# Where a transformer layer's output bias is added: GpSimd early, or VectorE in the last four expert groups

## The chip, the cores and the metric

One core of a Trainium2 chip runs the whole program. The metric is the device time of one launch in microseconds (us). The core has TensorE (PE), VectorE (DVE), ScalarE (ACT), GpSimd (POOL) and SyncE (SP), which here only issues transfers. Each engine works through its own instruction list in order, and the lists meet at semaphores.

## What the kernel computes

The input is x of 4 x 512 tokens and 256 channels. The result is x + attention(layernorm(x)) + experts(layernorm(x)), all in float32:

```
out  = einsum('bhqk,bkd->bhqd', softmax(q k^T * scale + window mask of 64), v)
attn = out.reshape(B, L, D) @ Wo + bo            # bo: 256 values, the bias this case is about
routed = einsum('ne,nef,efd->nd', comb, silu(x wg) * (x wu), wd)   # top 4 of 64 experts
shared = (silu(x swg) * (x swu)) @ swd
x = x + attn + routed + shared
```

The bias bo is a vector over the channels that is added to every token. It can be added at any place between x and the result.

## The kernel before

The 2048 tokens lie in 16 tiles (T) of 128, four for each of the four sequences (b). The stages, in the order of time:

1. **Head.** The four x blocks are loaded to `x_in[b]` (in the tile `wall`), normalized by DVE and ACT to `x_n[b]`, transposed and projected by PE. POOL rotates the queries of a tile (`rotate(T)`, four small operations, L1502 to L1508) and prepares the keys (`prepare_k`, L1478 to L1492).
2. **Attention turns, T = 0 to 15.** In each turn PE makes the scores of a tile twice (once to find the row maxima, which DVE reduces, L1110; once for the softmax), and the parts of three neighbouring tiles are in work at once. DVE also splits queries into bf16 parts (`leave`, L1104), copies keys (`near`, L1096), splits the maxima (L1119, L1121) and, in pieces set out by hand (`route_at`), works out the routing: top 4, ranks, the slots (L1230 writes `slot_i`). POOL sends each normalized tile four times to its experts' rows in DRAM (`scatter()`, L1518, an indirect DMA, 64 in all) with a rotation of tile T+4 in between. `SCATTERED_AT` says how many scatters a turn has: 4, in turns 12 and 13 six. From turn 1 on each scatter first waits for a step of PE.
3. **Base.** `add_x(T)` on DVE (L1155) adds x to the projected attention; the sum goes to DRAM (`base_d`). In the kernel before, x has had the bias added by then: `add_bias(b)` on POOL (L1575) adds `bo_sb` to the four tiles of `x_in[b]`, and `add_x` waits for it (`x_bo`).
4. **Expert groups, G = 0 to 31.** 127 blocks of 128 rows, four to a group. POOL copies the weights of each block's expert to a working buffer (L1545, up projection, buffers free when PE has used them; L1564, down projection). PE does `ups(G)` (L665), then `down(G-1)` (L690). Between them stand ACT's silu (L913) and DVE's `hidden(G)` (L1302, two products). `down(G)` begins only when all four down weights of its group are there. Results go to DRAM by ACT's copies (L926) and, in the last two groups, half by DVE (`copy_last_y`, L1309). The base rows are loaded back to `acc` in four parts of 512 KB (`load_base`), issued by SP in groups 24 to 27.
5. **Shared experts and sum.** PE does the shared experts (L604, L624). POOL fetches the four routed rows of each token (L1635, 64 indirect DMAs), DVE adds all (L1327, L1342) and SP stores the result.

## Time and profile before

| what | value |
|---|---|
| median of three runs | 370.13 us (370.11 to 371.2) |
| the profiled execution | 370.21 us |
| its span, first to last instruction | 368.9 us |
| PE busy | 336.3 us, 91% |
| POOL busy | 261.5 us, 71% |
| DVE busy | 252.4 us, 68% |
| ACT busy | 189.8 us, 51% |
| mean granted clock of TensorE | 0.986 of full |

The busy shares are means over stages with different limits. What a microsecond in one stage is worth is read from the chain of work that ended last, and from who waits for whom in that stage. 1.3 us of the execution's time lie outside the span.

### The profile page before, as it was taken

How to read it: one execution, taken by the hardware profiler on the slowest of the kernel's cores; microseconds unless marked ns; L12 is line 12 of the kernel's file. 1: busy time of each engine (PE TensorE's matmuls, PEld its weight loads, DVE VectorE, ACT ScalarE, POOL GpSimd, SP SyncE). 2: the span in 40 equal slices, each digit the busy share in tenths (PEclk: the TensorE clock that was granted, in tenths of full speed). 3: DMA queues.
4: the chain of work that ended last, by engine and by line, in shares of the span. 5: the costliest groups of instructions: out<-in, count | busy, mean ns of one | idle time of the engine just before them, and what ended most of it. 6: DMA issues, size and time to landing. Idle time of an engine off the chain costs nothing.

```text
span 368.9 us, 8678 instructions
## 1 busy us (share of the span) xinstructions
PE 336.3 (91%) x2710; PEld 250.6 (68%) x2711; DVE 252.4 (68%) x717; ACT 189.8 (51%) x359; POOL 261.5 (71%) x522
## 2 busy tenths in 40 slices
PE   6788589899898988899999999999999999999983
PEld 3676346566665565569999999999985466555572
DVE  4888899998898988645565464444444466677686
ACT  2595558898788876554555555555453111101100
POOL 6567988887777778525556657777773777777773
PEclk9999969999999999999999999999999999999998
DMA  8960233644494556679997883478985334444443
GB/s 246 231 159 4 72 109 114 199 159 147 143 267 156 155 173 182 176 223 221 348 320 226 273 267 115 173 239 276 294 278 180 107 114 132 130 124 129 128 142 114
DMA packets 73036, 66.81 MB, mean 181 GB/s; under 512 B 9053, under 2 KB 68701, under 8 KB 72993
## 3 DMA queue, kind: packets, MB, share of 16 engines
q1 hardware_dynamic: 66433, 49.30, 44.7%
q0 software_dynamic: 6144, 16.79, 14.4%
q8 instruction: 23, 0.38, 0.4%
q10 hardware_dynamic: 416, 0.18, 0.3%
q14 instruction: 20, 0.16, 0.1%
HBM read 36.78 MB, written 29.23 MB: 179 GB/s over the span
## 4 chain that ended last, share of the span: by engine, by line
PE 70%; DVE 16%; ACT 5%; issue 5%; DMA 2%; SPq 1%; DVEq 0%
PE bank L665 16%; PE bank L604 15%; PE bank L690 9%; PE bank L624 7%; PE bank L639 5%; PE bank L555 3%; PE bank L530 3%; DVE xall L1110 3%; PE bank L418 3%; PE bank L437 2%; DVE xall L1342 1%; PE bank L538 1%; DVE xall L1104 1%; DMA wdn<-edges 1%; DMA wall<-in_x 1%
## 5 line engine op out<-in xcount | busy, mean ns | idle before, releaser
L1635 POOL DMA_INDIRECT wall<-y_d,y_row x64 | 62.5, 977 | 26.0 <-issue 18.9
L1518 POOL DMA_INDIRECT xs_d<-spare,slot_i x64 | 64.7, 1012 | 19.2 <-issue 7.0
L1302 DVE TENSOR_TENSOR spare<-bank,spare 64x512 f32<-64x512 f32 (+1 forms) x64 | 44.1, 689 | 30.7 <-ACT spare L913 29.8
L665 PE MATMUL bank<-xall,spare 128*128 x508 | 63.9, 279 | 0.0
L665 PEld LDWEIGHTS bank<-xall,spare 128*128 128x128 f32 x508 | 59.4, 192 | 2.1
L1545 POOL COPY spare<-wall 128x256 f32 x127 | 48.0, 400 | 17.5 <-PE bank L665 9.8
L604 PE MATMUL bank<-xnT,xall 128*128 128x512 f32 x128 | 57.3, 594 | 0.0
L926 ACT ACTIVATE spare<-bank 128x512 f32<-128x512 f32 (+1 forms) x62 | 33.6, 593 | 28.7 <-PE bank L690 16.7
L604 PEld LDWEIGHTS bank<-xnT,xall 128*128 128x128 f32 x128 | 24.1, 190 | 25.1 <-issue 24.4
L872 ACT ACTIVATE xall<-bank 128x512 f32<-128x512 f32 x64 | 36.3, 599 | 8.1 <-PE bank L487 6.4
L889 ACT ACTIVATE xall<-bank 128x512 f32<-128x512 f32 x16 | 9.5, 597 | 59.6 <-PE bank L604 59.6
L864 ACT ACTIVATE xall<-bank 98x1024 bf16<-98x1024 bf16 x32 | 32.7, 1022 | 12.8 <-PE bank L437 11.5
L1342 DVE SCALAR_TENSOR_TENSOR xall<-wall,gate,xall 128x256 f32<-128x256 f32 x64 | 30.9, 485 | 2.3
L913 ACT ACTIVATE spare<-bank 64x512 f32<-64x512 f32 (+1 forms) x32 | 18.8, 587 | 25.1 <-PE bank L665 25.1
L624 PE MATMUL bank<-xall 128*128 128x256 f32 x128 | 29.7, 380 | 1.0 <-DVE xall L1327 1.0
L624 PEld LDWEIGHTS bank<-xall 128*128 128x128 f32 x128 | 24.3, 190 | 9.3 <-issue 5.3
L1172 DVE COPY xall<-bank 128x256 f32<-128x256 f32 x32 | 13.6, 424 | 24.8 <-PE bank L639 24.4
L855 ACT ACTIVATE xall<-xall 128x768 bf16<-128x768 f32 (+2 forms) x48 | 28.9, 625 | 1.6 <-DVE xall L1104 1.3
L1110 DVE TENSOR_REDUCE xall<-bank 128x4 f32<-128x316 f32 x64 | 27.9, 477 | 0.0
L487 PE MATMUL bank<-xall,wdn 128*128 128x256 bf16 x120 | 21.0, 278 | 6.3 <-ACT xall L872 4.2
L1316 DVE SCALAR_TENSOR_TENSOR xall<-xall,bank 128x512 f32<-128x512 f32 x16 | 11.0, 688 | 21.7 <-ACT xall L889 21.7
L1564 POOL COPY small<-wdn 128x128 f32 x24 | 7.0, 293 | 22.1 <-PE bank L690 21.9
(174 smaller groups left out, 640.8 us busy)
## 6 DMA issues: line engine op xcount, KB each, us to landing
y_d<-spare SPq DMA_DIRECT2D x31, 512.0 KB, 3.8
wall<-in_wg SPq DMA_DIRECT2D x16, 256.0 KB, 3.9
wall<-in_wu SPq DMA_DIRECT2D x16, 256.0 KB, 4.9
wdn<-in_wd SPq DMA_DIRECT2D x16, 256.0 KB, 4.6
spare<-xs_d SPq DMA_DIRECT2D x32, 128.0 KB, 3.4
small<-xs_d SPq DMA_DIRECT2D x32, 128.0 KB, 3.1
wall<-in_x SPq DMA_DIRECT2D x4, 512.0 KB, 5.5
base_d<-spare SPq DMA_DIRECT2D x16, 128.0 KB
```

Of the source, the lines that this page charges most:

```text
L604: ins = pe.matmul((gate_bank(i), up_bank(i))[half], wsh[:, c, half, ex, f0:f0 + P], xnT[:, c, g * GN:(g + 1) * GN], start=c == 0, stop=c = ...
L624: ins = pe.matmul(shared_bank(T), hs[T // GT % 2][:, k, t * P:(t + 1) * P], wshd[:, k, :], start=k == 0, stop=k == FC - 1)
L665: ins = pe.matmul(up_bank_of(G)[:, j * P:(j + 1) * P], wcur[i % NW][:, c * 2 * F:(c + 1) * 2 * F], x_half[c][:, bass.ds(o, P)], start=c == ...
L690: ins = pe.matmul(o[:, j * P:(j + 1) * P], hT[G % 2][rows64, j * P:(j + 1) * P], down_weights_of(G)[j][rows64, :], start=True, stop=True)
L872: act.activation(probs[n % 2][:, e * 512:(e + 1) * 512], bank[2 + e][:, :], ACT.Exp).then_inc(s["exp"], 1)
L926: act.activation(yb[G % 2][:, 0:n, half * P:(half + 1) * P], o[:, 0:n * P].rearrange("p (j d) -> p j d", d=P), ACT.Copy).then_inc(s["y_out ...
L1110: dve.tensor_reduce(maxf[T % 2][:, w * 8 + 4 * e:w * 8 + 4 * e + 4], bank[e][:, 0:4 * NEAR].rearrange("p (g n) -> p g n", g=4), AX.X, ALU.max,
L1302: ins = dve.tensor_tensor(hT[G % 2][half, 0:n], up_bank_of(G)[F:P, 0:n], sg[0:F, 0:n], ALU.mult)
L1342: dve.scalar_tensor_tensor(a, yk[:, T, k, :], gate[:, T, k:k + 1], a, ALU.mult, ALU.add).then_inc(s["sum"], 1)
L1518: pool.indirect_dma_start(out=xs_d, out_offset=bass.IndirectOffsetOnAxis(ap=slot_i[:, T, k:k + 1], axis=0), in_=x_n[b][:, t, :], in_offset ...
L1545: pool.tensor_copy(wcur[i % NW].rearrange("p (c g f) -> p c g f", c=NC, g=2), wall[:, bass.ds(o, WE)].rearrange("p (g c f) -> p c g f", c= ...
L1635: pool.indirect_dma_start(out=yk[:, T, k, :], out_offset=None, in_=of, in_offset=bass.IndirectOffsetOnAxis(ap=y_row[:, T, k:k + 1], axis=0 ...
```

## The change

POOL's 16 additions of the bias are gone, and with them DVE's wait for them. The bias is loaded later, by SP in group 18, to a row buffer that is free by then (`xrow[2]`), and DVE adds it to each of the four loaded parts of `acc` in groups 28 to 31, one operation of 128 x 1024 per group, behind `hidden(G)`. The fifth rotation, `rotate(4)`, moves from ahead of the scatters to between the four scatters of turn 0.

```diff
-    bo_sb = rt.take(D)
+    bo_late = xrow[2]
...
-    EXPERT_ROW, EXPONENTS = 13, 4
+    EXPERT_ROW, EXPONENTS, BIAS_AT = 13, 4, 18
...
         def add_x(T):
             dve.wait_ge(s["attended"], T + 1)
-            dve.wait_ge(s["x_bo"], T + 1)
...
+        def add_bias(b):
+            dve.wait_ge(s["bo"], 16)
+            dve.wait_ge(s[f"acc{b}"], 16)
+            a = acc[:, b * TPB:(b + 1) * TPB, :]
+            dve.tensor_tensor(a, a, bo_late.unsqueeze(1).to_broadcast([P, TPB, D]), ALU.add).then_inc(s["with_bo"], 1)
...
         def add_shared(T):
-            dve.wait_ge(s[f"acc{T // TPB}"], 16)
+            dve.wait_ge(s["with_bo"], T // TPB + 1)
...
+            if NGRP - B <= G < NGRP:
+                add_bias(G - (NGRP - B))
...
-        def add_bias(b):
-            pool.wait_ge(s["bo"], 16)
-            pool.wait_ge(s["normed"], (b + 1) * TPB // 2)
-            pool.wait_ge(s["normed_act"], (b + 1) * TPB // 2)
-            for t in range(TPB):
-                pool.tensor_tensor(x_in[b][:, t, :], x_in[b][:, t, :], bo_sb, ALU.add).then_inc(s["x_bo"], 1)
-                yield
...
         rotate_whole(3)
         prepare_k(3)
-        rotate_whole(4)
-        add_bias_whole(0)
-        add_bias_whole(1)
         slots = scatter()
         for T in range(NT):
-            if T == 0:
-                pieces = add_bias(2)
...
-                elif T == NT - TPB:
-                    pieces = add_bias(B - 1)
+            pieces = rotate(T + TPB) if T < NT - TPB else iter(())
...
-        sp.dma_start(bo_sb, bo.partition_broadcast(P)).then_inc(s["bo"], 16)
...
+            if G == BIAS_AT:
+                sp.wait_ge(s["g_T"], XB)
+                sp.dma_start(bo_late, bo.partition_broadcast(P)).then_inc(s["bo"], 16)
```

The instructions stand as follows. First POOL's list at the start of the scatters, before: the end of `prepare_k(3)`, `rotate(4)`, eight additions, then scatters with the additions of the third block between them.

```order
L1492 CAST xall<-xall 128x4x16
L1502 TENSOR_TENSOR xall<-xall,cf 128x128
L1504 TENSOR_TENSOR xall<-xall,cf 128x128
L1506 TENSOR_TENSOR xall<-xall 128x16x4
L1508 TENSOR_TENSOR xall<-xall 128x16x4
L1575 TENSOR_TENSOR wall<-wall,wdn 128x256 x8
L1518 DMA xs_d<-spare,slot_i 8192x256
L1575 TENSOR_TENSOR wall<-wall,wdn 128x256
L1518 DMA xs_d<-spare,slot_i 8192x256
```

The same place in the changed kernel, whose lines are numbered a little otherwise (L1525 is the scatter, L1509 to L1515 the rotation):

```order
L1499 CAST xall<-xall 128x4x16
L1525 DMA xs_d<-spare,slot_i 8192x256
L1509 TENSOR_TENSOR xall<-xall,cf 128x128
L1525 DMA xs_d<-spare,slot_i 8192x256
L1511 TENSOR_TENSOR xall<-xall,cf 128x128
L1525 DMA xs_d<-spare,slot_i 8192x256
L1513 TENSOR_TENSOR xall<-xall 128x16x4
L1525 DMA xs_d<-spare,slot_i 8192x256
L1515 TENSOR_TENSOR xall<-xall 128x16x4
```

So the first scatter stands right behind `prepare_k(3)`, and 12 additions are gone from here. Next POOL's list in turns 12 to 15, before: the last rotation, then the remaining scatters with the four additions of the fourth block.

```order
L1508 TENSOR_TENSOR xall<-xall 128x16x4
L1518 DMA xs_d<-spare,slot_i 8192x256
L1575 TENSOR_TENSOR wall<-wall,wdn 128x256
L1518 DMA xs_d<-spare,slot_i 8192x256 x4
L1575 TENSOR_TENSOR wall<-wall,wdn 128x256
L1518 DMA xs_d<-spare,slot_i 8192x256 x2
L1575 TENSOR_TENSOR wall<-wall,wdn 128x256
L1518 DMA xs_d<-spare,slot_i 8192x256 x4
L1575 TENSOR_TENSOR wall<-wall,wdn 128x256
L1518 DMA xs_d<-spare,slot_i 8192x256 x5
```

After the change sixteen scatters stand there with nothing between them. Last, DVE's list in groups 28 to 31 and behind them, in the changed kernel (L1301 is `hidden`, L1308 `copy_last_y`, L1315 the first operation of the shared experts):

```order
L1301 TENSOR_TENSOR spare<-bank,spare 64x512 x30
L1325 TENSOR_TENSOR xall<-xall,spare 128x1024
L1301 TENSOR_TENSOR spare<-bank,spare 64x512 x2
L1325 TENSOR_TENSOR xall<-xall,spare 128x1024
L1301 TENSOR_TENSOR spare<-bank,spare 64x512 x2
L1325 TENSOR_TENSOR xall<-xall,spare 128x1024
L1308 COPY spare<-bank 128x4x128
L1301 TENSOR_TENSOR spare<-bank,spare 64x384 x2
L1325 TENSOR_TENSOR xall<-xall,spare 128x1024
L1308 COPY spare<-bank 128x3x128
```

The rows L1325 are the new additions; the third stands ahead of the first `copy_last_y`, the fourth ahead of the second. Nothing else on DVE has moved, and PE's list is the same in both.

## Rows read from the trace of the kernel before

**Rows 1.** The chain that ended last, its last long piece: start us, us, what

```profile
355.30 7.19 PE bank L624 x32
```

**Rows 2.** The chain that ended last, 28 to 70 us

```profile
38.15 0.88 DVE xall L1104
...
40.93 0.78 DVE slot_i L1230
41.71 0.84 DVE wdn L1096
...
47.39 0.77 DVE slot_i L1230
...
49.40 0.67 DVE xall L1121
...
51.96 1.91 PE bank L530 x16
```

**Rows 3.** POOL's timeline: start us, us, engine, line, what

```profile
38.02 5.78 POOL L1575 TENSOR_TENSOR wall<-wall,wdn 128x256 f32<-128x256 f32 x8
...
47.36 0.74 POOL L1575 TENSOR_TENSOR wall<-wall,wdn 128x256 f32<-128x256 f32 x1
...
49.28 0.74 POOL L1575 TENSOR_TENSOR wall<-wall,wdn 128x256 f32<-128x256 f32 x1
```

**Rows 4.** Single lines of DVE: duration ns min/median/max, first and last start us

```profile
L1104 DVE TENSOR_TENSOR xall<-xall x32: 409/416/991, 19.6 to 140.7; 128x256 f32<-128x256 f32 x32
L1096 DVE COPY wdn<-xall x16: 310/328/909, 27.1 to 149.7; 98x640 bf16<-98x640 bf16 x16
L1121 DVE TENSOR_TENSOR xall<-xall x16: 174/214/659, 36.0 to 154.2; 128x16 bf16<-128x16 f32 x16
L1230 DVE TENSOR_SCALAR slot_i<-wdn x2: 765/770/776, 40.9 to 47.4; 128x32 int32<-128x32 f32 x2
```

**Rows 5.** Timelines of POOL and DVE, a scatter beside a small DVE operation

```profile
57.03 0.98 POOL L1518 DMA_INDIRECT xs_d<-spare,slot_i  x1 [0.17 <-issue]
57.40 0.59 DVE L1119 CAST xall<-xall 128x16 bf16<-128x16 f32 x1
```

**Rows 6.** Timelines of DVE and POOL in turns 13 and 14

```profile
137.82 0.70 DVE L1104 TENSOR_TENSOR xall<-xall 128x256 f32<-128x256 f32 x1
140.68 0.73 POOL L1575 TENSOR_TENSOR wall<-wall,wdn 128x256 f32<-128x256 f32 x1
140.71 0.99 DVE L1104 TENSOR_TENSOR xall<-xall 128x256 f32<-128x256 f32 x1
```

**Rows 7.** Timelines of POOL and DVE, a 128 x 1024 addition beside a rotation

```profile
67.55 1.41 POOL L1504 TENSOR_TENSOR xall<-xall,cf 128x128 f32<-128x128 f32 x1
67.48 1.23 DVE L1248 TENSOR_TENSOR wdn<-wdn,small 128x1024 f32<-128x1024 f32 x1
```

**Rows 8.** Timelines of PE, DVE and POOL, groups 29 and 30

```profile
273.53 1.16 PE L690 MATMUL bank<-spare 64*128 64x128 f32 x16
271.19 1.40 DVE L1302 TENSOR_TENSOR spare<-bank,spare 64x512 f32<-64x512 f32 x2 [1.35 <-ACT spare L913]
269.80 0.40 POOL L1545 COPY spare<-wall 128x256 f32 x1
271.19 1.00 POOL L1564 COPY spare<-wdn 128x128 f32 x4
```

**Rows 9.** The DMA view: a transfer's issues, KB each, median us to landing

```profile
xall<-base_d SPq DMA_DIRECT2D x4, 512.0 KB, 6.8
```

**Rows 10.** Timeline, the end of the last group

```profile
280.97 0.75 PEld L690 LDWEIGHTS bank<-spare 64*128 64x128 f32 x12 [0.85 <-DVE spare L1302]
281.99 0.56 DVE L1309 COPY spare<-bank 128x384 f32<-128x384 f32 x1 [1.07 <-PE bank L690]
```

**Rows 11.** Windows: us, busy us (count) of PE, PEld, DVE, ACT, POOL, granted clock, DMA share, GB/s

```profile
48.00:49.00 1.00, 1.00 (x4) 0.39 (x2) 0.97 (x4) 0.44 (x1) 0.83 (x2) 0.50 0.24 86
...
53.00:54.00 1.00, 0.97 (x11) 0.15 (x4) 0.81 (x4) 1.00 (x3) 0.80 (x3) 0.50 0.57 169
```

More of the change, by code:

```diff
@@ L116 @@
     "stats moments var scaled rs normed biased route member totals_read rank_read slots rows "
-    "q_left diag wslice shifted gate k_out k_near o_out max mpart max_out rden a_tok ah hs h y_out_dve gT_dve expert_read with_x based sum "
-    "v_fill fill prep roped k_split weights down_weights x_bo "
+    "q_left diag wslice shifted gate k_out k_near o_out max mpart max_out rden a_tok ah hs h y_out_dve gT_dve expert_read with_x with_bo based sum "
+    "v_fill fill prep roped k_split weights down_weights "
 ).split() + [f"fetched{T}" for T in range(NT - 1)] + [f"last_fetched{k}" for k in range(TOPK)]
@@ L1331, in sum_up @@
             if T in SUM_FIRST:
-                dve.wait_ge(s[f"acc{T // TPB}"], 16)
+                dve.wait_ge(s["with_bo"], T // TPB + 1)
             else:
@@ L1568, in gpsimd @@
         pool.wait_ge(s["c32"], 16)
-        def add_bias(b):
-            pool.wait_ge(s["bo"], 16)
-            pool.wait_ge(s["normed"], (b + 1) * TPB // 2)
-            pool.wait_ge(s["normed_act"], (b + 1) * TPB // 2)
-            for t in range(TPB):
-                pool.tensor_tensor(x_in[b][:, t, :], x_in[b][:, t, :], bo_sb, ALU.add).then_inc(s["x_bo"], 1)
-                yield
-        def add_bias_whole(b):
-            for _ in add_bias(b):
-                pass
         def rotate_whole(T):
@@ L1593, in gpsimd @@
         prepare_k(3)
-        rotate_whole(4)
-        add_bias_whole(0)
-        add_bias_whole(1)
         slots = scatter()
         for T in range(NT):
-            if T == 0:
-                pieces = add_bias(2)
-                for i in range(SCATTERED_AT(T)):
-                    next(slots)
-                    next(pieces)
-            else:
-                if T < NT - TPB:
-                    pieces = rotate(T + TPB)
-                elif T == NT - TPB:
-                    pieces = add_bias(B - 1)
-                for i in range(SCATTERED_AT(T)):
+            pieces = rotate(T + TPB) if T < NT - TPB else iter(())
+            for i in range(SCATTERED_AT(T)):
+                if T > 0:
                     if i < 2:
@@ L1616, in gpsimd @@
                         pool.wait_ge(s["weighted"], QB * (T - 1) + min(i, 4) - 2)
-                    next(slots, None)
-                    if T < NT - TPB or i in (0, 4):
-                        next(pieces, None)
+                next(slots, None)
+                next(pieces, None)
         for _ in slots:
```

## The prediction

> **What bounds the kernel now.** I read the chain that ended last first, because the page's busy shares hide which engine counts in which stage. From about 160 us to 362 us the chain is PE almost without a gap; its last long piece is a run of 32 products of 7.19 us [rows 1]. In that stretch work taken off POOL gains nothing by itself; what matters is only whether something new makes PE wait. From 28 to 70 us it is otherwise. There DVE's routing steps stand on the chain [rows 2], and so do a few of them again in turns 13 and 14. All POOL additions that the change removes lie in these two stretches. Every engine behind them is paced by turns, with no transfer found waiting at a fixed time, so a microsecond gained there should reach the end.
>
> The next view is the timeline of POOL beside that of DVE. POOL is not waited for in the early stretch, yet it costs time. Eight additions run back to back from 38.02 us, 0.72 us each [rows 3], and the DVE operations under them are long: L1104 takes 0.88 us on the chain, L1230 0.78, L1096 0.84 [rows 2]. The view of single lines gives their usual lengths, 0.416 us for L1104, 0.328 for L1096, 0.174 at the least for L1121 [rows 4]. L1230 runs twice and takes 0.77 both times, each time with an addition of POOL under it, so its free length is not in the trace. The ends tell the mechanism. Additions at 0.7225 us each from 38.02 have an end at 40.91 and one at 41.63; L1230 starts at 40.93 and ends at 41.71, just behind the second. The single additions at 47.36 and 49.28 [rows 3] end at 48.10 and 50.02, and the DVE operations over them end at 48.16 and 50.07 [rows 2]. DVE waits until POOL's instruction is done. The two engines hold something in turns, not side by side.
>
> The Trainium skill (SBUF — State Buffer, "Who interferes with whom") has a rule for that: the two engines share one pair of ports to the memory, held as a lock for a whole instruction, and a VectorE operation with two inputs in SBUF is in its way only against a GpSimd instruction that reads there. The trace agrees with the lock for whole instructions.
>
> **Part by part, the gain.** (a) *Turn 0, 38 to 42.5 us.* After the change POOL has nothing between the end of `prepare_k(3)`, 36.6 us, and the first scatter, which must wait for L1230. So three waits go: L1104 0.88 - 0.42 = 0.46; L1230 0.78 less its free length; L1096 0.84 - 0.33 = 0.51. For L1230 the nearest free row is L1121's 0.174 (128 x 16, also a tiny operation), which gives 0.60. Its bounds are 0 (all of its 0.77 is its own) and 0.60. The sum is 1.57; I take 1.5, as L1096 now meets the start of the first scatter. Low end 0.7, high end 1.6. ACT does not catch it: its table load in this stretch hangs on PE's transposes, which L1104 also holds up.
>
> (b) *Turn 1, 45 to 51 us.* The second L1230 and L1121 lose the additions under them: 0.60 and 0.67 - 0.17 = 0.50, together 1.1. But scatters come in their place, since POOL reaches turn 1 about 5 us earlier. A scatter also holds DVE: L1119 takes 0.59 beside one instead of some 0.17 [rows 5], so 0.4 a hit. I take half, 0.5, between 0 (both meet one again) and 1.1. The skill's rule, taken at its word, frees L1121 (two inputs) from scatters that only write descriptors, and would put this term at 0.7; the sum goes by the row.
>
> (c) *Turns 12 to 14.* L1104 is at 0.70 and at 0.99 with additions of the fourth block under it [rows 6], against 0.42: 0.28 + 0.57 = 0.85. I take 0.8, between 0.2 (the scatters that move forward collide in their place) and 1.0.
>
> (d) *At nothing:* the moved rotation. `rotate(4)` ends at some 47 us instead of 38, and is needed by ACT only in turn 2, after 51 us; the cover is 4 us. Also the wait `x_bo` in `add_x`, which had always been met; and the 128 KB load that leaves the head of SP's queue. In group 18 SP issues that load ahead of one y store: less than a microsecond of SP's time, which idles about 2 us in each group there; behind it only y stores are queued, for which ACT has a group's time.
>
> The gain is 1.5 + 0.5 + 0.8 = 2.8 us, with ends at 0.9 and 3.7.
>
> **The price.** (e) Four additions of 128 x 1024 on DVE. The same shape took 1.23 us [rows 7]. DVE's own time hides them: between `hidden(29)`, done at 271.19 + 1.40 = 272.59, and `hidden(30)` about 3.1 us after 271.19 there are 1.7 us. What they wait for is there: the `acc` parts are issued four groups ahead, 12 us, against 6.8 us to landing [rows 9]. But they have both inputs in SBUF and hold POOL, whose weight copies feed PE. The row for it is L1504, which took 1.41 us instead of 0.41 under L1248 [rows 7]: held until the addition ends. I follow the first two on POOL's timeline. The addition of group 28 is due at 269.83, just after POOL's copy at 269.80 [rows 8] has begun, so it starts at about 270.15 and ends at 271.3. POOL's two remaining copies for `ups(30)` come at 271.3 and 271.65, needed by PE in `ups(30)`, the 2.0 us ahead of 273.53, at 272.5 and 273.0: no stall. The four down weights of group 29, before at 271.19 to 272.19 [rows 8], now begin at 272.0, one each 0.24 us. The fourth is due at 272.71, and the second addition of DVE is due at 272.7. If DVE is first, that copy ends at 274.1, while `down(29)` is due at 273.53 [rows 8] and waits for all four: a PE stall of 0.6. If POOL is first, nothing. In group 30 the same meeting falls at 275.6 to 275.7 and has 0.5 us at stake. In group 31 POOL has finished. I put 0.5 for the two, between 0 and 1.2.
>
> (f) In group 31 `hidden` ends as PE needs it, PE waits for it [rows 10], and nothing is put ahead of it. The addition behind it, 280.92 to 282.1, delays the last y copy, due at 281.99 [rows 10], by 0.1 us, and with it the fetches of the routed rows, which POOL issues nearly without a pause up to the end. I put 0.1.
>
> The sum against the execution's own time: 370.21 - 2.8 + 0.6 = 368.0 us, 0.6% below the median of 370.13, from which the execution differs by 0.08.
>
> The Trainium skill (VectorE: DVE Perf Modes, fp32 formula for an add of two tensors) gives (1024 + 151)/0.96 = 1224 ns for the new addition, an estimate; the trace agrees with its 1.23 us. Its lock for whole instructions speaks against this change: by it POOL stands still for nearly 4 x 1.2 us in the groups, and only POOL's slack keeps this from PE.
>
> **Rivals.** *The scatters take the additions' place* (0.17). The DVE waits of turns 1 and 12 to 14 stay, and L1230 is slow by itself. For it: rows 5, and no free L1230 in the trace. Against it: in turn 0 no scatter can start before L1230. Gain 0.9, price 0.6: 369.9, within what can't be told.
>
> *The clock does not fall* (0.13). The granted clock is 0.50 at 48 us and still at 53, the lower of TensorE's levels, 1.2 against 2.4 GHz [rows 11], after PE had stood idle for much of 40 to 48 us waiting for DVE. With the waits gone it may stay up. PE's 16 products of L530 took 1.91 us at that level [rows 2], about 0.95 too long; with the transposes ahead of them it is some 1.3 us, of which DVE, busy at 0.8 to 0.97, lets perhaps 1.0 through: 367.0 us. Against it: PE still idles most of those microseconds.
>
> *The clock falls at a worse time* (0.09), the case on the slow side. If the fall comes in turns 2 to 4, where PE is busy nearly all the time, and lasts twice the present six microseconds, it costs up to half its length, 6 us, less the 1.3 of the present one and what DVE would hide: some 4 us, and 368.0 + 4.0 = 372.0 us. It decides against the change from about 3.3 us of added cost, that is, 6.6 us more of half clock over work bound by PE. Against it: the early idling shrinks, so nothing asks for more.
>
> *The additions hold POOL more than worked out* (0.08): both meetings lost and the gain at its middle, 368.7 us, still faster.
>
> *The forecast* has 0.53, with its own range 367.2 to 368.8.
>
> **How the numbers follow.** A measurement of this kernel tells about 0.3%, 1.1 us: faster is below 369.0. Forecast, high clock and lost meetings give 0.74, of which some spills over 369.0; I put faster at 0.70, same at 0.20, slower at 0.10. The range reaches up to the first rival and down to the second: 366.7 to 369.9.
>
> **What would show it.** L1104 of turn 0 at 0.42 us, the first L1230 at about 0.2, the first scatter near 41 us and not 44; turn 1's L1230 and L1121 shorter on average by a half; L1104 of turn 14 at 0.42; the four additions at 1.2 us each in groups 28 to 31, POOL's copies beside them late by about 1 us, and a gap ahead of `down(29)` of 0 or 0.6. I am wrong if L1230 stays at 0.77 with no POOL instruction under it, if the interval to 160 us shrinks by less than 1 us, or if PE's run through the last four groups grows by more than 1.2 us.

## The result, and the profile after

The changed kernel takes 366.2 us, the median of 15 runs (363.9 to 369.2), beside 370.2 us for the kernel before on the same chip (15 runs, 368.4 to 372.6). The ratio is 0.989, with an interval of 0.987 to 0.991: 4.0 us or 1.1% faster. The forecast was 2.1 us less, with a range of 0.2 to 3.4 us less. The direction was right and the size too small: the result lies outside the range.

The profiled execution of the changed kernel took 367.16 us, 3.05 us less than that of before. It is slower than the median by about 1 us. From its start to turn 0 it is 0.6 us behind that of before (the first pair of L1110 reductions of turn 0's routing starts at 35.41 us, before at 34.82), where the change only takes the bias load away; with that load back, in `head_load`, the pair starts at 35.27. Net of that, the part that the change touches is 3.6 us shorter, near the difference of the medians. The lines moved by one: L1230 of before is L1229 now, the scatter is L1525, the rotation L1509 to L1515, the new addition L1325, the weight copies on POOL L1552 and L1571.

First the page's busy time and clock.

```profile
PE 336.9 (92%) x2711; PEld 251.1 (69%) x2711; DVE 252.1 (69%) x721; ACT 190.2 (52%) x359; POOL 252.2 (69%) x506
PEclk9999969999999999999999999999999999999998
```

The timeline of DVE in turns 0 and 1 (start us, us, engine, line), which answers to [rows 2]:

```profile
38.45 0.42 DVE L1104 TENSOR_TENSOR xall<-xall 128x256 f32<-128x256 f32 x1
...
40.77 0.18 DVE L1229 TENSOR_SCALAR slot_i<-wdn 128x32 int32<-128x32 f32 x1
40.86 0.32 DVE L1096 COPY wdn<-xall 98x640 bf16<-98x640 bf16 x1
...
43.99 0.67 DVE L1104 TENSOR_TENSOR xall<-xall 128x256 f32<-128x256 f32 x1 [1.51 <-ACT xall L855]
...
46.44 0.35 DVE L1229 TENSOR_SCALAR slot_i<-wdn 128x32 int32<-128x32 f32 x1
...
47.90 0.17 DVE L1121 TENSOR_TENSOR xall<-xall 128x16 bf16<-128x16 f32 x1
...
52.50 0.69 DVE L1136 COPY xall<-bank 128x512 f32<-128x512 f32 x1 [0.86 <-PE bank L530]
```

The three operations that waited for POOL in turn 0 have their free lengths: 0.42, 0.18 and 0.32 us. L1096 now ends at 41.18 us instead of 42.55. The last row is new: in turn 1 DVE waits 0.86 us for PE. It waits for the 16 products of L530, which took 1.91 us before [rows 2] and take 1.86 now, from 50.57 us on. The windows say that the clock still falls, only earlier (the last three columns are the granted clock, the DMA share and GB/s):

```profile
46.00:47.00 1.00, 0.53 (x4) 0.47 (x4) 0.96 (x6) 0.91 (x2) 0.81 (x3) 0.50 0.07 29
...
50.00:51.00 1.00, 1.00 (x14) 0.63 (x16) 0.93 (x3) 0.85 (x3) 1.00 (x1) 0.50 0.34 111
```

It is back at 1.00 from 53 us on.

POOL's timeline, which answers to [rows 3]: nothing stands between `prepare_k(3)` and the first scatter, and the rotation's pieces lie between the scatters.

```profile
41.84 1.19 POOL L1525 DMA_INDIRECT xs_d<-spare,slot_i  x1 [4.58 <-DVE slot_i L1229]
...
43.64 1.02 POOL L1525 DMA_INDIRECT xs_d<-spare,slot_i  x1 [0.17 <-issue]
...
46.40 0.34 POOL L1513 TENSOR_TENSOR xall<-xall 128x64 f32<-128x64 f32 x1
```

Set one beside the other: L1229 at 46.44 to 46.79 us and the rotation at 46.40 to 46.74 end together. The rotation now holds DVE where it stands. L1104 at 43.99 has become longer too, 0.67 us instead of 0.43. It ends at 44.66 with the scatter that began at 43.64, behind which the next piece of the rotation stands.

DVE in turn 13, which answers to [rows 6]:

```profile
136.07 0.42 DVE L1104 TENSOR_TENSOR xall<-xall 128x256 f32<-128x256 f32 x1
...
138.26 0.18 DVE L1121 TENSOR_TENSOR xall<-xall 128x16 bf16<-128x16 f32 x1
138.35 0.42 DVE L1104 TENSOR_TENSOR xall<-xall 128x256 f32<-128x256 f32 x1
```

Both L1104 are free, and so is an L1121 that took 0.61 us before, which the forecast hadn't counted. Last, the expert groups. DVE and POOL in groups 28 and 29:

```profile
265.07 1.40 DVE L1301 TENSOR_TENSOR spare<-bank,spare 64x512 f32<-64x512 f32 x2 [1.67 <-ACT spare L913]
266.50 1.44 DVE L1325 TENSOR_TENSOR xall<-xall,spare 128x1024 f32<-128x1024 f32 x1
268.14 1.40 DVE L1301 TENSOR_TENSOR spare<-bank,spare 64x512 f32<-64x512 f32 x2 [0.20 <-ACT spare L913]
269.57 1.34 DVE L1325 TENSOR_TENSOR xall<-xall,spare 128x1024 f32<-128x1024 f32 x1
271.21 1.40 DVE L1301 TENSOR_TENSOR spare<-bank,spare 64x512 f32<-64x512 f32 x2 [0.30 <-ACT spare L913]
```

```profile
266.47 2.42 POOL L1552 COPY spare<-wall 128x256 f32 x4 [0.37 <-PE bank L665]
268.84 1.00 POOL L1571 COPY spare<-wdn 128x128 f32 x4
...
269.55 0.29 POOL L1571 COPY spare<-wdn 128x128 f32 x1
```

PE, down products of group 29 and the first wide product behind group 30's (before they started at 273.53 [rows 8] and 274.62 us):

```profile
264.33 1.16 PE L690 MATMUL bank<-spare 64*128 64x128 f32 x16
...
270.48 1.16 PE L690 MATMUL bank<-spare 64*128 64x128 f32 x16
271.57 1.98 PE L604 MATMUL bank<-xnT,xall 128*128 128x512 f32 x4
```

From `down(27)` to `down(29)` it is 6.15 us, before too (267.38 to 273.53), and 1.09 us on to L604 in both. PE has no gap: in this execution the four additions cost it nothing. POOL's copies are held (four L1552 in 2.42 us), but it has the time. It was close, though. The row at 269.55, asked for alone, is the last of the four copies of down weights at 268.84. `down(29)` needs it, and it began 0.02 us ahead of the addition at 269.57. The experiments show executions in which the addition came first. The lead of 3.05 us at 271.57 is the same as at PE's last long piece, 352.25 us instead of 355.30 [rows 1].

The offsets give the change by stages. Start to turn 0: 0.59 later. At the end of the first L1096: 1.37 earlier, so turn 0 gave 1.96. At 62 us: 1.52, so turn 1 gave 0.15. It stays between 1.5 and 1.55 through turn 11. At the pair of turn 15: 2.86, and behind the turns 3.05, so turns 12 to 15 gave 1.5. Behind that: nothing. Together 3.6 us.

### The profile page after: what moved, and what is told of

Its sections match the earlier page's. It is cut to its first block, busy times and chain, and to the rows that moved or that the text cites. A ratio compares the mean times of both kernels' runs of the same rounds, so it can differ in the third digit from the quotient of the medians.

```text
span 365.8 us, 8665 instructions
## 1 busy us (share of the span) xinstructions
PE 336.9 (92%) x2711; PEld 251.1 (69%) x2711; DVE 252.1 (69%) x721; ACT 190.2 (52%) x359; POOL 252.2 (69%) x506
## 4 chain that ended last, share of the span: by engine, by line
PE 76%; DVE 12%; ACT 6%; issue 4%; POOL 1%; DVEq 0%; POOLq 0%
PE bank L665 16%; PE bank L604 15%; PE bank L690 10%; PE bank L624 7%; PE bank L639 5%; PE bank L530 4%; PE bank L555 4%; DVE xall L1110 4%; PE bank L418 3%; PE bank L437 3%; PE bank L406 2%; PE bank L487 2%; DVE xall L1347 1%; PE bank L538 1%; ACT xall L872 1%
## 5 line engine op out<-in xcount | busy, mean ns | idle before, releaser
L1525 POOL DMA_INDIRECT xs_d<-spare,slot_i x64 | 64.6, 1010 | 27.0 <-PE bank L487 7.2
L1301 DVE TENSOR_TENSOR spare<-bank,spare 64x512 f32<-64x512 f32 (+1 forms) x64 | 44.1, 689 | 27.9 <-ACT spare L913 27.0
L1552 POOL COPY spare<-wall 128x256 f32 x127 | 49.9, 416 | 17.9 <-PE bank L665 10.0
L604 PE MATMUL bank<-xnT,xall 128*128 128x512 f32 x128 | 57.3, 594 | 0.0
L604 PEld LDWEIGHTS bank<-xnT,xall 128*128 128x128 f32 x128 | 24.1, 190 | 25.1 <-issue 24.4
L1110 DVE TENSOR_REDUCE xall<-bank 128x4 f32<-128x316 f32 x64 | 27.9, 477 | 0.0
L1315 DVE SCALAR_TENSOR_TENSOR xall<-xall,bank 128x512 f32<-128x512 f32 x16 | 11.0, 688 | 21.5 <-ACT xall L889 21.5
L1571 POOL COPY small<-wdn 128x128 f32 x24 | 7.0, 293 | 22.9 <-PE bank L690 22.8
```

Source lines behind the costliest of these rows:

```text
L604: ins = pe.matmul((gate_bank(i), up_bank(i))[half], wsh[:, c, half, ex, f0:f0 + P], xnT[:, c, g * GN:(g + 1) * GN], start=c == 0, stop=c = ...
L1110: dve.tensor_reduce(maxf[T % 2][:, w * 8 + 4 * e:w * 8 + 4 * e + 4], bank[e][:, 0:4 * NEAR].rearrange("p (g n) -> p g n", g=4), AX.X, ALU.max,
L1301: ins = dve.tensor_tensor(hT[G % 2][half, 0:n], up_bank_of(G)[F:P, 0:n], sg[0:F, 0:n], ALU.mult)
L1525: pool.indirect_dma_start(out=xs_d, out_offset=bass.IndirectOffsetOnAxis(ap=slot_i[:, T, k:k + 1], axis=0), in_=x_n[b][:, t, :], in_offset ...
L1552: pool.tensor_copy(wcur[i % NW].rearrange("p (c g f) -> p c g f", c=NC, g=2), wall[:, bass.ds(o, WE)].rearrange("p (g c f) -> p c g f", c= ...
```

## The experiments

There were eighteen runs. In fourteen of them (all but the one group of four) every execution, those of the kernel before too, took 384 to 400 us, but for one of 652 us. In their profiles ScalarE stood still three or more times, for up to 16 us, nearly always in the shared-expert stage, which no edit touches; there only profiles and large differences are read. One row of the first run, of ACT in the shared-expert stage, where the idle time ended with nothing that the trace holds:

```profile
337.51 1.08 ACT L889 ACTIVATE xall<-bank 128x512 f32<-128x512 f32 x2 [14.38 <-remote]
```

### The halves of the change, undisturbed

One group of four on one chip, three rounds: the changed kernel again, its two halves, and the rotation put back. The kernel before took 370.92 us there (22 executions; `late_all` and `rotate_ahead` have 6 each, `early_late` 11, `last_late` 12). `early_late` is the changed kernel with the fourth block's additions left on POOL in turns 12 to 14:

```diff
+            elif T == NT - TPB:
+                pieces = pool_bias(B - 1)
...
-            if NGRP - B <= G < NGRP:
+            if NGRP - B <= G < NGRP and G - (NGRP - B) in (0, 1, 2):
```

`last_late` leaves the first three blocks' additions on POOL, ahead of the scatters and between them in turn 0, with `rotate(4)` ahead of them as before, and adds only the fourth block late:

```diff
+        rotate_whole(4)
+        for b in range(2):
+            for _ in pool_bias(b):
+                pass
...
+            if T == 0:
+                pieces = pool_bias(2)
...
+            if NGRP - B <= G < NGRP and G - (NGRP - B) in (3,):
```

`rotate_ahead` is the changed kernel with only the rotation moved back:

```diff
+        rotate_whole(4)
         slots = scatter()
...
-            pieces = rotate(T + TPB) if T < NT - TPB else iter(())
+            pieces = rotate(T + TPB) if 0 < T < NT - TPB else iter(())
```

> The changed kernel on a third chip. In the two sets before, all kernels took 385 to 396 us, the kernel before too, with pauses of ScalarE of 14 us each in the shared experts that end on nothing in the trace; there its gain over the kernel before was not seen. Where such pauses are absent, port theory: 3.6 us under the kernel before (ratio 0.990). Where they are there, a difference of 1 to 3 us between kernels is not told apart, whatever the theory.

> Additions of sequences 0 to 2 on VectorE late, those of sequence 3 on GpSimd in turns 12 and 13. Without pauses: 2.1 us under the kernel before (port theory, turns 0 and 1 alone), or 3.6 us (order theory: what counts is when the scatters start).

> Additions of sequence 3 alone on VectorE late. Without pauses: 1.5 us under the kernel before (port theory, turns 12 to 14 alone), or under 0.5 us (order theory). The earlier run of this kernel had L1231 at 0.77 us and L1097 at 0.91 us in turn 0 as the kernel before, which the port theory needs, and I expect both again.

> The changed kernel with the fifth rotation put back ahead of the scatters. I costed the move at nothing. Port theory: its four two-input operations of 0.3 to 0.4 us fall on VectorE's small operations at 37 to 38.5 us, which cost 0.1 to 0.3 us there, and in return the scatters of turns 0 and 1 run closer together; together within 0.3 us of the changed kernel. If the move is what gives the gain, 1 us or more slower than it.

| kernel | median us | ratio to before, interval | turn 0's pair to turn 1's | turn 12's to turn 15's |
|---|---|---|---|---|
| before | 370.92 | | 8.1 | 21.9 |
| `late_all` | 366.13 | 0.9877 [0.9844, 0.9911] | 6.2 | 20.6 |
| `early_late` | 368.45 | 0.9935 [0.9911, 0.9958] | 6.2 | 21.9 |
| `last_late` | 368.77 | 0.9942 [0.9917, 0.9967] | 7.6 | 20.6 |
| `rotate_ahead` | 365.19 | 0.9855 [0.9823, 0.9887] | 6.4 | 20.6 |

The last two columns are us between the starts of L1110's pairs of reductions, from each profile. The halves are worth 2.5 and 2.15 us, together 4.6 of the whole's 4.8. In the stretches of the additions each half gains where its own additions are gone: `early_late` 2.0 us in turn 0 and nothing in turns 12 to 15, `last_late` 1.3 us in turns 12 to 15. `last_late` also gains 0.5 us in turn 0, where the additions stand as before: its L1105 began at 39.95 us, ahead of the first addition at 40.10, and took 0.47 us instead of 0.88; here the addition waited (0.92 us). So not all of its 2.15 us belongs to the fourth block. Outside these stretches single profiles differ by 1 to 2 us as well, by the clock in turn 1 and by waits of PE, both below. The DVE rows of `early_late`, with POOL's one addition (here L1594) beside them:

```profile
40.76 0.18 DVE L1232 TENSOR_SCALAR slot_i<-wdn 128x32 int32<-128x32 f32 x1
...
136.69 0.61 DVE L1122 TENSOR_TENSOR xall<-xall 128x16 bf16<-128x16 f32 x1
137.23 0.98 DVE L1105 TENSOR_TENSOR xall<-xall 128x256 f32<-128x256 f32 x1
```

```profile
136.20 0.96 POOL L1537 DMA_INDIRECT xs_d<-spare,slot_i  x1 [0.30 <-issue]
137.17 0.74 POOL L1594 TENSOR_TENSOR wall<-wall,wdn 128x256 f32<-128x256 f32 x1
```

And those of `last_late`, where it is the reverse:

```profile
42.33 0.77 DVE L1231 TENSOR_SCALAR slot_i<-wdn 128x32 int32<-128x32 f32 x1
43.02 0.91 DVE L1097 COPY wdn<-xall 98x640 bf16<-98x640 bf16 x1
...
139.13 0.42 DVE L1105 TENSOR_TENSOR xall<-xall 128x256 f32<-128x256 f32 x1
```

At these places the waits of DVE come and go with POOL's additions. The rival, that the gain is from the scatters' earlier start, falls: in `early_late` the first scatter starts at 41.82 us, as early as with the whole change, and it has only half the gain, with turns 12 to 15 as long as before. L1121 (L1122 here) at 0.61 us belongs to the additions: it is there in before and in `early_late`, and 0.17 to 0.18 in all that have no addition behind that scatter. It ends 0.14 us behind the scatter's end, so whether the scatter or the addition next in POOL's queue holds it isn't settled.

**The rotation.** With it back ahead, the kernel is 0.9 us faster by the medians of six executions each (365.19 beside 366.13; the intervals overlap), where I had put it within 0.3 us. The move gains nothing in time. The profiles show what it trades. Ahead, the rotation lengthens a few operations of turn 0 (L1217 takes 0.33 us, with the move 0.20), and turn 0 is 6.4 us long instead of 6.2. Moved, it stands over turn 1's: from turn 1's first pair of reductions to its second it is 4.54 us in `rotate_ahead` (41.60 to 46.14) and 5.10 in `late_all` and in the first profile of the changed kernel, 5.12 before. So the move costs 0.56 us there and gives back 0.2. DVE of `rotate_ahead`:

```profile
43.84 0.43 DVE L1104 TENSOR_TENSOR xall<-xall 128x256 f32<-128x256 f32 x1 [1.35 <-ACT xall L855]
...
46.05 0.18 DVE L1229 TENSOR_SCALAR slot_i<-wdn 128x32 int32<-128x32 f32 x1
...
47.25 0.17 DVE L1121 TENSOR_TENSOR xall<-xall 128x16 bf16<-128x16 f32 x1
47.35 0.42 DVE L1104 TENSOR_TENSOR xall<-xall 128x256 f32<-128x256 f32 x1
```

and POOL's beside them:

```profile
45.88 0.96 POOL L1525 DMA_INDIRECT xs_d<-spare,slot_i  x1 [0.31 <-issue]
47.15 0.96 POOL L1525 DMA_INDIRECT xs_d<-spare,slot_i  x1 [0.30 <-issue]
```

L1229, L1121 and L1104 each began within the first 0.2 us of a scatter here and ran at their free lengths. But scatters do hold DVE elsewhere. In the changed kernel's turn 13, where only scatters are left on POOL, a cast of 128 x 16 that takes 0.17 us free is held until the scatter's end:

```profile
137.29 0.96 POOL L1525 DMA_INDIRECT xs_d<-spare,slot_i  x1 [0.30 <-issue]
137.94 0.29 DVE L1119 CAST xall<-xall 128x16 bf16<-128x16 f32 x1
```

The L1119 of [rows 5] is the same case with more of the scatter left (0.59 us). The two-input L1104 was held in a scatter when a piece of the rotation came next on POOL (0.67 us at 43.99 in the changed kernel), and wasn't when another scatter came next (0.43 us at 43.84 here). One row of the second kind is too few, and so it stays likely and not shown.

**The clock.** Between 44 and 55 us it fell to 0.50 in five of the six undisturbed profiles (before, the changed kernel and these four), at other times and for other lengths; in `early_late` not at all in this stretch. Its window, beside that of the changed kernel above:

```profile
50.00:51.00 1.00, 0.83 (x21) 0.36 (x10) 0.91 (x4) 1.00 (x3) 1.00 (x1) 1.00 0.32 107
```

From turn 1's pair to turn 2's it took 9.8 us there, 10.2 in `rotate_ahead` and 10.7 in `late_all` (0.50 for 3.4 us in both; they differ by the rotation), 11.7 in the first profile of the changed kernel and 11.8 in before (0.50 for 6.8 us in both). So the fall costs up to 2.0 us of the kernel's time, and it differs between executions of one kernel: `late_all` is the changed kernel. Part of what separates medians from one pair of profiles lies here.

**The additions and `down(29)`.** `early_late` makes three of the late additions, and there the addition of group 29 came ahead of POOL's fourth copy of down weights. The four copies took 1.99 us instead of 1.00, and PE waited for the last:

```profile
270.32 1.23 DVE L1328 TENSOR_TENSOR xall<-xall,spare 128x1024 f32<-128x1024 f32 x1
```

```profile
269.71 1.99 POOL L1583 COPY spare<-wdn 128x128 f32 x4
```

```profile
271.80 1.16 PE L691 MATMUL bank<-spare 64*128 64x128 f32 x16 [0.49 <-issue]
```

The trace names no releaser for this wait, but the fourth copy ends at 271.70 us. It is the stall of 0.6 us that the prediction put under "if DVE is first". Of the eleven profiles with one late addition in group 29 (the execution of 652 us left aside), six have it, 0.49 to 0.51 us each (`early_late`, `again`, `whole_5`, `pool_3`, `head_load`, `dead_copies_5`), and five don't. No profile without late additions in group 29 has it, before's included. Two of the six are the changed kernel itself. In `early_late` PE also waited 0.80 us for a DMA at 174.29 us, so its gain in one profile is understated by both.

### The same halves, and the late additions, in disturbed groups

The first group held the changed kernel again, both halves, and one without any late addition (the output bias is then left out):

```diff
-                add_bias(G - (NGRP - B))
+                pass
```

> The changed kernel once more, on the chip that the other kernels of this set run on. Theory 1, port: its gain is made of waits of VectorE for GpSimd's additions, 1.9 us in turn 0, 0.2 in turn 1 and 1.5 in turns 12 to 14 by the two traces, and nothing is lost in the groups, so it is 3.6 us under the kernel before (ratio 0.990). Theory 2, head: part of the 3.9 us between the medians is the bias load that left the head of the queue; then the first projection of this kernel (first L418) stands earlier than before's 13.76 us. The one profile so far has it 0.6 us later at 28 us, which theory 1 takes for scatter between executions.

> Only the additions of sequences 0 to 2 move to VectorE; the four of sequence 3 stay on GpSimd in turns 12 and 13, and the bias is loaded both at the head and late. Port theory: the gain of turns 0 and 1 alone, 2.1 us under the kernel before, and L1104 of turn 14 back at 0.9 us or more. Rival, order: the gain comes from the scatters starting and ending earlier, so nearly all of the 3.6 us stays with this kernel, since its scatters start as early.

> Only the additions of sequence 3 move to VectorE; those of sequences 0 to 2 stay on GpSimd ahead of and between the first scatters, with the fifth rotation ahead of them. Port theory: the gain of turns 12 to 14 alone, 1.5 us under the kernel before. Rival, order: nothing under 0.5 us, since the scatters start as late as before.

> The changed kernel without the four additions on VectorE in groups 28 to 31, so that the output lacks the bias. What I predicted for their price was 0.6 us; the trace of the changed kernel shows none, since GpSimd's fourth down copy of group 29 was in before the addition. Price nil: within 0.2 us of the changed kernel. Price as predicted: 0.6 us faster than it, in the interval from ups(29) to the first product of the shared experts.

Ratios to before: `again` 1.0013 [0.9976, 1.0050], `pool_3` 0.9904 [0.9862, 0.9946], `pool_012` 1.0062 [1.0022, 1.0103], `no_late_add` 0.9965 [0.9925, 1.0005], with the kernel before at 391.5 us. By these the first half is faster than the whole, and the whole is no faster than the kernel before. The undisturbed group says otherwise. Whether the stops swallow the gain isn't known: there is no profile of the kernel before with stops. So the gain of 1.1 to 1.2% is shown where ScalarE runs undisturbed, and there alone.

The additions were then measured against one another on one chip, five rounds: the changed kernel, one without them, and one in which each is made twice (the output has the bias twice):

```diff
+            dve.wait_ge(s["with_bo"], 2 * b + 1)
+            dve.tensor_tensor(a, a, both, ALU.add).then_inc(s["with_bo"], 1)
```

> The changed kernel with each of the four late additions made twice in a row (the output has the bias twice). Two hold the port for 2.5 us of a group's 3.07, and VectorE has 1.7 us free between two hidden steps, so hidden(29), hidden(30) and the down weights come late: 0.8 us in each of groups 29 and 30, 0.5 in group 31, in all 2 us over the changed kernel. If the additions cost nothing for want of anyone who waits, under 0.5 us.

> The changed kernel itself, beside which the other three of this group are read. Lock theory: 3.5 to 4.8 us less than the kernel before (0.987 to 0.991). Rival, that the gain seen so far is mostly the varying stretch of half clock in turn 1: 1.5 to 2.5 us (0.993 to 0.996).

> The changed kernel without the four VectorE additions of the last expert groups: the output bias is not added at all. If these additions are hidden, as PE's unbroken run through the last groups says, it takes the same time as the changed kernel beside it, within 0.4 us. If they cost what the forecast put on them, 0.6 us, it is 0.5 us or more faster.

> The changed kernel with each of the four late additions made twice (the output holds the bias twice). VectorE and, by the lock, GpSimd's weight copies stand still another 1.2 us in each of groups 28 to 31. If the cover of one addition is all there is, PE stops by 0.5 to 1 us in three or four groups: 2 to 4 us more than the changed kernel beside it. If the cover is ample, nothing.

> The changed kernel without the four late additions: the output bias is left out. Hidden, as PE's unchanged cadence through the last groups says: the time of the changed kernel, 0.985 to 0.991 of the kernel before. At the forecast's price: 0.6 us less than the changed kernel.

`double_add` gave 1.0148 [1.0095, 1.0200]. In the later group `whole_5` took 390.89 us, 1.0003 [0.9967, 1.0038]; `late_none_5` 391.17, 0.9995 [0.9962, 1.0029]; `late_twice_5` 393.42, 1.0108 [1.0063, 1.0152]. `late_none_3` gave 0.9972 [0.9932, 1.0012]. That `whole_5` equals the kernel before is against both theories put down for it, and it is the second such result with `again`, on another chip. Within the group, no additions and one each take the same time (0.3 us apart, less than the intervals tell), two each cost 2.5 us. PE of `late_twice_5` shows where:

```profile
277.92 1.16 PE L690 MATMUL bank<-spare 64*128 64x128 f32 x16 [0.83 <-DVE spare L1301]
...
281.87 0.49 PE L690 MATMUL bank<-small,spare 64*128 64x128 f32 x4 [0.88 <-DVE spare L1301]
```

1.7 us of waits for `hidden`, L1301: with two additions DVE itself is late, and not only POOL's copies, which the forecast had feared. That fits the idle time left before L1301 in the changed kernel, 0.20 and 0.30 us of a period of 3.07.

### The head's load, and what in a POOL operation holds DVE

`head_load` puts a dead 128 KB load back at the head of SP's queue. `dummy_memset` and `dummy_copy` put dead POOL operations, two each, in the sixteen places of the removed additions, with the rotation ahead of them again and the real additions still late; `dead_copies_5` and `dead_copies_3` are `dummy_copy` again:

```diff
+        sp.dma_start(bo_sb, bo.partition_broadcast(P)).then_inc(s["bo_early"], 16)
```

```diff
+                    dummy(lambda: pool.memset(bo_sb, 0.0))
```

```diff
+                    dummy(lambda: pool.tensor_copy(bo_sb.rearrange("p (i n) -> p i n", i=2), ident.unsqueeze(1).to_broadcast([P, 2, P])))
```

> The changed kernel with the bias load at the head of SP's queue kept beside the late one (its result is not read). Head theory: 0.3 us slower than the changed kernel or more, as x blocks 2 and 3 share the engines with 128 KB in 1 KB rows. Port theory: the same as the changed kernel to 0.2 us.

> The changed kernel, but GpSimd has in each of the 16 old places of an addition two memsets of 128 x 256 into a buffer that nobody reads (0.3 us each, so some 0.7 us in the place of 0.72), and the fifth rotation stands ahead of them again. The bias is still added late. Rule of the port page (a two-input VectorE operation is in the way only of GpSimd instructions that read SBUF): L1104 and L1121, two inputs, run at 0.42 and 0.17 us under them, while the copies and the tensor-scalar operations (L1230, L1096), if they use the shared pair, still wait; gain between 1.5 and 2.5 us of the 3.6. Rival, any GpSimd instruction holds VectorE: as slow as the kernel before to 0.5 us. Rival, only scatter order counts: as slow as the kernel before too, but with L1104 of turn 0 at 0.42.

> As the kernel with memsets, but with two copies of 128 x 256 out of the identity matrix (0.4 us each), which read SBUF as the additions do. Port theory: VectorE waits for them as for additions, with a little less at a time since each lasts 0.4 us and not 0.72; 0 to 1.5 us under the kernel before, slower than the one with memsets. If the length of one GpSimd instruction does not matter, the same as before.

> The changed kernel with two dead one-input copies of 128 x 256 on GpSimd in each of the sixteen places where an addition of 0.72 us stood, the additions themselves still late on VectorE. Theory of two inputs: only a GpSimd instruction with two inputs in memory holds VectorE, so the routing steps stay short and the time stays within 1 us of the changed kernel's. Rival, that any GpSimd work in those places costs (its own time puts the scatters and rotations off, or it holds VectorE too): 2 to 4 us more than the changed kernel.

> The changed kernel with two dead one-input copies of 128 x 256 on GpSimd (0.94 us together) in each of the sixteen places where an addition of 0.72 us stood. If only instructions with two inputs in memory hold VectorE: routing steps near their free length, a time within 1.5 us of the changed kernel's (0.984 to 0.992 of the kernel before). If GpSimd's mere occupation there costs what the additions cost: no faster than the kernel before (0.997 to 1.005).

Ratios to before: `head_load` 1.0010 [0.9980, 1.0039], `dummy_memset` 0.9984 [0.9945, 1.0023], both as `whole_5` on that chip; `dummy_copy` 1.0083 [1.0044, 1.0123], `dead_copies_5` 1.0036 [1.0000, 1.0071], `dead_copies_3` 0.9895 [0.9792, 0.9997] of four runs. In time this stays open: by the ratios the copies of `dead_copies_5` cost 1.3 us beside `whole_5`, with overlapping intervals. The profile that was to show the memsets is the execution of 652.49 us; it is read for a single row below. The profiles are clear on the waits. DVE of `dead_copies_3`, and POOL's sixteen copies over them:

```profile
38.12 0.47 DVE L1105 TENSOR_TENSOR xall<-xall 128x256 f32<-128x256 f32 x1
...
40.51 0.24 DVE L1230 TENSOR_SCALAR slot_i<-wdn 128x32 int32<-128x32 f32 x1
40.66 0.32 DVE L1097 COPY wdn<-xall 98x640 bf16<-98x640 bf16 x1
```

```profile
38.27 7.90 POOL L1588 COPY wdn<-cf 128x256 f32<-128x256 f32 x16
```

POOL is busy almost without a pause, and the three operations take 0.47, 0.24 and 0.32 us where the additions made them 0.88, 0.78 and 0.84. It looks as if one-input copies held nothing. The ends say otherwise. Two pairs, the first from turn 1 of `dead_copies_3`, the second from turn 1 of `dummy_copy`:

```profile
45.76 0.40 POOL L1588 COPY wdn<-cf 128x256 f32<-128x256 f32 x1
45.83 0.37 DVE L1230 TENSOR_SCALAR slot_i<-wdn 128x32 int32<-128x32 f32 x1
```

```profile
45.08 0.40 POOL L1588 COPY wdn<-cf 128x256 f32<-128x256 f32 x1
45.10 0.66 DVE L1105 TENSOR_TENSOR xall<-xall 128x256 f32<-128x256 f32 x1 [1.35 <-ACT xall L856]
```

L1230 ends 0.04 us behind the copy, as it ended 0.04 to 0.05 behind an addition in the kernel before (41.71 beside 41.67, 48.15 beside 48.10). L1105 ends 0.27 us behind the copy, and its twin L1104 ended 0.29 behind the additions (39.03 beside 38.74, 138.52 beside 138.23, 141.70 beside 141.41). A copy holds DVE just as an addition does, until its own end. It costs less because it is shorter, 0.40 us instead of 0.72, and because of where the operations fell: the L1105 at 38.12 began ahead of the first copy, at 38.27, and L1097 at 40.66 with 0.05 us of a copy left. The theory put down for `dead_copies_5`, that only two-input instructions hold DVE, falls; that of `dummy_copy`, waits as under additions and shorter, is what the rows show. As for instructions that only write, there is one row, in the memset run: an L1105 that began at 51.45 us, 0.02 into a memset of 0.31 us, took its free 0.43 us.

The copies cost POOL's own time too: the first scatter starts at 46.59 us instead of 41.84.

## Why the prediction was right in direction and too small

The mechanism stands: DVE waited for POOL's additions, and these waits are what the change gives back. The sum was 2.8 less 0.6; the profiles show 3.6 less 0. What failed are the sizes of terms. The largest error is (c), turns 12 to 14: 0.8 put, 1.5 measured, because a wait of L1121 was left out. Then (e), 0.5 put and 0 met in this execution, and (a), 1.5 put and 1.96 measured. (b) was off the other way.

- **(a) Turn 0**, 1.5, measured 1.96. The three waits gave 0.46, 0.60 and 0.59. The term that was missed is 0.3 us ahead of L1104 (from the pair of reductions to it 3.33 us before, 3.04 now): the moved rotation's own operations, from 36.6 us, had held the small operations there. L1230's free length, unknown before, is 0.18 us, at the bound that I took.
- **(b) Turn 1**, 0.5, measured 0.15 in the first profile. The waits shrank by more than I put: L1229 to 0.35 and L1121 to 0.17, 0.9 us together. They didn't reach the end. The 0.42 of L1229 is gone by the second pair of reductions already (5.12 us from the first before, 5.10 now), with L1104 longer by 0.24 and starting 0.16 later behind its pair; `rotate_ahead`, at 4.54, has this back, so it is the moved rotation that took it. Behind the second pair PE was at half clock and DVE waited for L530. I had let the gain through there without asking what PE would do at 0.50. The scatters, which I charged with the other half, can hold DVE, as [rows 5] said; here the rotation cost more.
- **(c) Turns 12 to 14**, 0.8, measured 1.5. This is the step that failed most. I counted 0.28 and 0.57 for the two L1104 and left L1121's 0.61 us between them out, giving it to the scatter under it. With 0.43 for it, and 0.12 for an L1104 in turn 12 (0.54 before, 0.42 now), the sum is 1.40.
- **(d) Nothing** for the head's load and the `x_bo` wait: no run contradicts it. For the rotation I looked only at who needs its result, and that was right; I didn't look at whom its operations hold, in the old place and in the new. Put at nothing, the move costs 0.56 us in turn 1 and gives back 0.2 in turn 0.
- **(e) The four additions**, 0.5, measured 0. My timeline had DVE's second addition meet POOL's fourth copy of down weights, and so it did. POOL was first by 0.02 us: the copies ended at 269.84 and the addition, at 269.57, took 1.34 us. That was luck. The mechanism was right, and in six of eleven profiles the meeting was lost at 0.49 to 0.51 us of PE's time, about the 0.6 worked out. Whichever came first could not be told from before. Over these profiles the meeting cost 0.27 us on average. DVE's own time is the next limit, with some 0.2 to 0.3 us left.
- **(f) The last y copy**, 0.1. The copy is 0.2 us late against PE (2.83 us ahead of before's 281.99, PE 3.05), and that costs nothing: the lead is 3.05 us behind it too.

With these, 370.21 - 3.6 + 0.6 (the late start) = 367.2, the execution's 367.16. Without the late start it is 366.6, near the median of 366.2.

The rivals: *the scatters take the additions' place* falls: its L1230, slow by itself, is 0.18 us free, and the waits of turns 12 to 14 went with the additions. *The clock does not fall* happened in one profile of six, and is worth up to 2.0 us, not the 1.0 that I put on it, as from turn 1's pair to turn 2's PE is what DVE waits for. *The clock falls at a worse time* was not seen. *The additions hold POOL more* is half seen: POOL's L1552 are held as forecast (2.42 us for four instead of 1.74), but this rival had both meetings lost, and no profile shows more than the one ahead of `down(29)`.

The Trainium skill (SBUF — State Buffer, "Who interferes with whom") says that a VectorE operation with two inputs in SBUF is in the way only of GpSimd instructions that read there, and that descriptor generation needs the pair for writing (the latter is inferred there). I set it aside in (b) for the row of L1119. The L1119 of [rows 5], a cast, belongs by the same section to the operations that can take both ports, and scatters hold it in this trace (0.59 us, 0.29 us at 137.94). `rotate_ahead` agrees on L1121 and L1104, two inputs each, which run inside scatters at 0.17 and 0.42 us. By the section's rule a copy on GpSimd, which reads, holds such an L1104, and `dummy_copy` agrees: 0.66 us, ending with the copy. A memset, which only writes, doesn't, and the one row there is agrees with that (0.43 us).

## What to carry to other kernels

Where two engines wait for each other's instructions, price every operation of the one that stands over the chain of the other, in the old place and the new, by what is left of it when the other's operation begins, and not by its busy time: here a hit under a 128 x 256 addition of 0.72 us cost 0.3 to 0.6 us, under a copy of 0.40 us up to 0.24, and a scatter held some operations and let others through. Short instructions hold little. Work taken off such a chain can be put where the engine waits for another one every period, as long as the idle time ahead of the next needed operation holds it: 1.67 us of DVE's took a 1.23 us addition, and not a second one. Then ask whom the moved work holds in its turn; here it was a weight copy that PE needs, a matter of 0.02 us in one execution and 0.5 us lost in others. I would keep `rotate_ahead`: the additions late, the rotation ahead of the scatters, 365.2 us, 0.9855 [0.9823, 0.9887] of the kernel before. That it beats the changed kernel is likely by its rows and not shown by the times.

## What the runs showed of the hardware that I had not expected

A tiny operation on DVE (128 x 32) takes 0.18 us free and 0.77 when it meets the start of a GpSimd addition of 0.72 us; under copies of 0.40 us it took 0.24 and 0.37. In every one of these it ends 0.03 to 0.05 us behind the GpSimd instruction, whether that has one input or two. The fall of the granted clock to 0.50 around 48 us differs between executions of one code: 6.8 us in one profile, 3.4 us in another, and in one variant none in that stretch. And on three of the chips ScalarE stood still for up to 16 us at a time, at operations that nothing in the trace releases, which added some 20 us to every kernel, before and after alike; what it waits for there is not known.
